# Transposing fp32 activation rows by one fp16 hi/lo DMA per item instead of four TensorE transposes

## The reference, cut to what matters

```
h   = layernorm(x)                                  # per row, eps 1e-5
z   = h @ ctx[e].T                                  # e = min(id clipped to 24999 // 6250, 3)
y   = (silu(z) * z) @ ctx[e]                        # Wg, Wu and Wd are all ctx, einsum 'bsf,df->bsd'
x   = x + tanh(g_xattn) * y
h2  = layernorm(x)
ffn = h2 @ W_base + b_base + (h2 @ A_s) @ B_s
      + sum over the top 2 of 6 experts: gate_e * (h2 @ A_r[e]) @ B_r[e]
out = x + tanh(g_ffn) * ffn
```

## Time and profile before

| | |
|---|---|
| time, median of 3 runs | 231.47 us (231.07 to 231.64) |
| span of the profiled execution, first to last instruction | 229.7 us |
| time of the profiled execution itself | not recorded apart from the runs above; their median lies 1.8 us over the span |
| mean granted TensorE clock | 0.990 of full speed |
| TensorE matmuls busy | 211.8 us (92% of the span) |
| TensorE weight loads busy | 181.7 us (79%) |
| VectorE busy | 168.1 us (73%) |
| ScalarE busy | 77.2 us (34%) |
| POOL busy | 95.4 us (42%) |

### The profile page before, as it was taken

How to read it: one execution, slowest core, us unless ns; L and a number is a source line. 1 busy time by engine, 2 the same in 40 slices (tenths; PEclk the granted TensorE clock), 3 DMA queues, 4 the chain that set the end, 5 groups by cost and what they waited for, 6 DMA issues and landing times.

```text
span 229.7 us, 4143 instructions
## 1 busy us (share of the span) xinstructions
PE 211.8 (92%) x1203; PEld 181.7 (79%) x1204; DVE 168.1 (73%) x423; ACT 77.2 (34%) x166; POOL 95.4 (42%) x147
## 2 busy tenths in 40 slices
PE   0666999999999999999999999999999999999990
PEld 0325788888888888888888889999999999999990
DVE  5878787777865666555566566768999989999761
ACT  4554334323422122222222216044333344333330
POOL 4887743332223333332100111116666665556742
PEclk9997999999999999999999999999999999999998
DMA  4986082111111111001100000001111111211122
GB/s 126 376 248 212 1 288 72 45 46 46 46 46 46 46 46 40 13 39 46 46 0 0 0 0 0 3 1 47 49 46 46 46 46 46 83 54 46 46 93 91
DMA packets 5994, 15.00 MB, mean 65 GB/s; under 512 B 1073, under 2 KB 1073, under 8 KB 5986
## 3 DMA queue, kind: packets, MB, share of 16 engines
q0 software_dynamic: 2800, 9.18, 12.4%
q1 hardware_dynamic: 2544, 4.21, 5.4%
q10 hardware_dynamic: 642, 1.52, 2.0%
HBM read 10.71 MB, written 4.19 MB: 65 GB/s over the span
## 4 chain that ended last, share of the span: by engine, by line
PE 75%; DVE 10%; issue 6%; POOL 5%; ACT 1%; DMA 1%; POOLq 1%; DVEq 0%
PE z_ps L466 17%; PE y_ps L466 17%; PE y_ps L471 8%; PE z_ps L471 8%; PE hT_ps L476 6%; PE ffn_b L466 4%; PE actT_ps L476 4%; PE ffn_a L466 3%; POOL xg L278 2%; PE ffn_b L471 2%; PE actT_ps L552 2%; DVE bn L845 2%; PE ffn_a L471 2%; POOL lo_onehot L294 2%; DVE hwT L893 1%
## 5 line engine op out<-in xcount | busy, mean ns | idle before, releaser
L269 POOL TENSOR_SCALAR var_eps<-stats 128x1 f32<-128x1 f32 x35 | 7.0, 201 | 107.6 <-DVE stats L757 107.4
L466 PE MATMUL z_ps<-ct_split,hT 128*128 x144 | 39.3, 417 | 1.2 <-ACT hT L349 1.2
L466 PE MATMUL y_ps<-ct_split,actT 128*128 x152 | 39.7, 403 | 0.0
L466 PEld LDWEIGHTS z_ps<-ct_split,hT 128*128 128x128 f32 x144 | 26.7, 195 | 6.5 <-issue 1.5
L466 PEld LDWEIGHTS y_ps<-ct_split,actT 128*128 128x128 f32 x152 | 27.2, 189 | 5.2 <-ACT actT L357 0.2
L357 ACT ACTIVATE actT<-actT_ps 128x512 fp32r<-128x512 f32 x19 | 11.4, 599 | 44.8 <-PE actT_ps L476 44.8
L772 DVE TENSOR_TENSOR act<-z_ps,silu 128x512 f32<-128x512 f32 x18 | 12.5, 692 | 17.8 <-ACT silu L353 17.4
L278 POOL DMA_INDIRECT xg<-x_rows,row_index x19 | 22.4, 1180 | 5.8 <-POOL rstd L272 4.2
L476 PE MATMUL hT_ps<-ident,h 128*128 128x128 f32 x140 | 21.1, 273 | 3.0 <-DVE h L761 3.0
L476 PEld LDWEIGHTS hT_ps<-ident,h 128*128 128x128 f32 x140 | 17.6, 142 | 6.2 <-DVE h L761 3.5
L353 ACT ACTIVATE silu<-z_ps 128x512 f32<-128x512 f32 x18 | 10.8, 599 | 34.3 <-PE z_ps L471 34.3
(11 more groups left out here) (157 smaller groups left out, 419.4 us busy)
## 6 DMA issues: line engine op xcount, KB each, us to landing
ct_stage<-ct SPq DMA_DIRECT2D x4, 1024.0 KB, 8.2
ct_stage<-w_ffn ACTq DMA_DIRECT2D x1, 1260.0 KB
xg<-x_rows,row_index POOLq DMA_INDIRECT x19, 3.6
out<-xg,row_index POOLq DMA_INDIRECT x16
ct_stage<-w_up ACTq DMA_DIRECT2D x1, 226.0 KB
ids_sb<-ids SPq DMA_DIRECT2D x1, 8.0 KB, 1.6
gates_raw<-gates SPq DMA_DIRECT2D x1, 1.0 KB, 2.7
br<-b_router SPq DMA_DIRECT2D x1, 3.0 KB
```

The lines of the kernel that those rows point to most:

```text
L466: nc.tensor.matmul(ps, lhs[:, 0, at], rhs(part), start=(k == 0 and part == 0), stop=False)
```

## The change

Each item's rows are split before they are transposed. `item_norm` writes one of two buffers `hs`, scaled by 2^10 (the factor goes into the root). ScalarE rounds it to fp16 (`h_hi`), VectorE writes the difference in fp16 beside it (`h_lo`), and one transposing DMA from SyncE moves the 128 x 1024 halves into `hT_half`, eight blocks of 128 x 128. ScalarE widens all of it in one instruction into the fp32r operand pair, with the scale taken back (`widen`). The TensorE transposes of h, `hT_hi` and `hT_lo` go away in the item stage; product z waits once, for `hT_ready`. The Fori loops of ScalarE and VectorE are written out, TensorE's goes in steps of two. The order becomes:

```diff
         @block.sync
...
-            for q in range(ITEMS):
+            for q in range(3):
                 sp.wait_ge(x_landed[q], 16)
                 sp.sem_inc(x_ready, 1)
+            for q in range(ITEMS):
+                sp.wait_ge(h_lo_ready, q + 1)
+                sp.dma_start_transpose(hT_half[q % 2][:], h_split[q % 2][:]).then_inc(hT_landed[q % 2], 16)
+                if q + 3 < ITEMS:
+                    sp.wait_ge(x_landed[q + 3], 16)
+                    sp.sem_inc(x_ready, 1)
...
-                root(n, rstd_ready, 4 + n + 1)
+                root(n, rstd_ready, 4 + n + 1, 2.0 ** (-2 * H_POWER))
...
-            def hT_hi(q, to=hT):
-                act_e.wait_ge(hT_done, q + 1)
-                nc.scalar.activation(to[:, 0], hT_ps[:], ACT.Copy).then_inc(hT_hi_ready, 1)
+            def h_hi(q):
+                act_e.wait_ge(h_ready, q + 1)
+                nc.scalar.activation(h_split[q % 2][:, 0:D], hs[q % 2][:], ACT.Copy).then_inc(h_hi_ready, 1)
+
+            def widen(q):
+                act_e.wait_ge(hT_landed[q % 2], 16 * (q // 2 + 1))
+                nc.scalar.activation(hTs[q % 2][:].rearrange("p a n -> p (a n)"),
+                                     hT_half[q % 2][:].rearrange("p b t -> p (b t)"), ACT.Copy,
+                                     scale=2.0 ** -H_POWER).then_inc(hT_ready, 1)
...
-            def item(q):
-                silu_of(q)
-                hT_hi(q + 1)
+            def item(q, bank=z_ps):
+                silu_of(q, bank)
+                if q + 2 < ITEMS:
+                    h_hi(q + 2)
                 actT_hi(q)
+                if q + 2 < ITEMS:
+                    widen(q + 2)
...
-            hT_hi(0)
+            h_hi(0)
+            h_hi(1)
+            widen(0)
             ct_hi(LATE_KEY, 0)
             ct_hi(LATE_KEY, 1)
-            hT_hi(1, to=hT_1)
-            silu_of(0)
-            actT_hi(0)
+            widen(1)
+            item(0)
...
-            def product_z(q):
+            def product_z(q, slot):
                 key = key_of(q)
                 pe.wait_ge(ct_lo_ready, S)
-                pe.wait_ge(hT_hi_ready, q + 1)
-                expert_hi(z_ps, hT, key)
-                pe.wait_ge(hT_lo_ready, q + 1)
-                expert_lo(z_ps, hT, key).then_inc(z_done, 1)
+                pe.wait_ge(hT_ready, q + 1)
+                expert_hi(z_ps, hTs[slot], key)
+                expert_lo(z_ps, hTs[slot], key).then_inc(z_done, 1)
...
-            with pe.Fori(2, ITEMS - 1) as q:
-                product_z(q)
-                transpose_h(q + 1)
-                product_y(q - 1)
-                transpose_act(q)
+            with pe.Fori(2, ITEMS - 1, 2) as q:
+                for slot in range(2):
+                    product_z(q + slot, slot)
+                    product_y(q + slot - 1)
+                    transpose_act(q + slot)
...
-            def hT_lo(q, to=hT):
-                dve.wait_ge(hT_hi_ready, q + 1)
-                tt(to[:, 1], hT_ps[:], to[:, 0].bitcast(F32), ALU.subtract).then_inc(hT_lo_ready, 1)
+            def h_lo(q):
+                dve.wait_ge(h_hi_ready, q + 1)
+                tt(h_split[q % 2][:, D:], hs[q % 2][:], h_split[q % 2][:, 0:D], ALU.subtract
+                   ).then_inc(h_lo_ready, 1)
...
             def item(q, bank=z_ps, first=False, extra_before=False):
...
                 aggregate(stats_ready)
-                hT_lo(q + 1)
                 if first:
                     gates_of_rows()
                 item_norm(q + 2)
                 add_product(q - 1, target_of(q - 1) if extra_before else q - 1)
                 actT_lo(q)
+                h_lo(q + 2)
```

More of the change, by code:

```diff
@@ L87, in build_block @@
         h2T = [hT, hT_1, actT]
+        hTs = (hT, hT_1)
+        hs = (h, sb("h_1", [P, D]))
+        h_split = [sb(f"h_split{slot}", [P, 2 * D], F16) for slot in range(2)]
+        hT_half = [sb(f"hT_half{slot}", [P, 2 * KC, P], F16) for slot in range(2)]
         hw = sb("hw", [P, LORA + 1])
@@ L178, in build_block @@
         stats_ready, rstd_ready, h_ready = sem("stats_ready"), sem("rstd_ready"), sem("h_ready")
-        hT_done, hT_hi_ready, hT_lo_ready = sem("hT_done"), sem("hT_hi_ready"), sem("hT_lo_ready")
+        h_hi_ready, h_lo_ready, hT_ready = sem("h_hi_ready"), sem("h_lo_ready"), sem("hT_ready")
+        hT_landed = [sem(f"hT_landed{slot}") for slot in range(2)]
         z_done, silu_ready, act_ready = sem("z_done"), sem("silu_ready"), sem("act_ready")
@@ L205, in build_block @@
         CONSTS = 12
+        H_POWER = 10
         def cols(tensor, position, width=D):
@@ L265, in _, with root @@
             pool.wait_ge(consts_ready, CONSTS)
-            def root(n, done, step):
-                nc.gpsimd.tensor_scalar(var_eps[:], stats[:, 1:2], EPS, 1.0, ALU.add, ALU.mult
+            def root(n, done, step, divisor=1.0):
+                nc.gpsimd.tensor_scalar(var_eps[:], stats[:, 1:2], EPS, divisor, ALU.add, ALU.mult
                                         ).then_inc(pool_step, 1)
@@ L397, in _ @@
             act_e.dma_start(up_stage, w_up).then_inc(up_loaded, 16)
-            silu_of(1, z_1_ps)
-            hT_hi(2)
-            actT_hi(1)
+            item(1, z_1_ps)
             act_e.wait_ge(w_loaded, 16)
-            with act_e.Fori(2, 2 + KC) as q:
+            for q in range(2, 2 + KC):
                 item(q)
@@ L406, in _ @@
             nc.scalar.activation(up_split[:, 0], up_stage, ACT.Copy).then_inc(w_hi_ready, 1)
-            with act_e.Fori(2 + KC, ITEMS - 1) as q:
+            for q in range(2 + KC, ITEMS - 1):
                 item(q)
@@ L492, in key_of @@
                 return pe.value_load(key_table[0:1, bass.ds(q, 1)], min_val=0, max_val=S - 1)
-            def transpose_h(q):
-                pe.wait_ge(h_ready, q + 1)
-                transpose_chunks(hT_ps, h).then_inc(hT_done, 1)
-            def product_z(q):
+            def product_z(q, slot):
                 key = key_of(q)
                 pe.wait_ge(ct_lo_ready, S)
-                pe.wait_ge(hT_hi_ready, q + 1)
-                expert_hi(z_ps, hT, key)
-                pe.wait_ge(hT_lo_ready, q + 1)
-                expert_lo(z_ps, hT, key).then_inc(z_done, 1)
+                pe.wait_ge(hT_ready, q + 1)
+                expert_hi(z_ps, hTs[slot], key)
+                expert_lo(z_ps, hTs[slot], key).then_inc(z_done, 1)
             def product_y(q, key=None, bank_used=True, between=None):
@@ L568, in product_up @@
                 last.then_inc(up_done, 1)
-            transpose_h(0)
             pe.wait_ge(tables_ready, 1)
@@ L577, in _ @@
             pe.wait_ge(ct_lo_ready, key_0 + 1)
-            pe.wait_ge(hT_hi_ready, 1)
+            pe.wait_ge(hT_ready, 1)
             expert_hi(z_ps, hT, key_0)
-            transpose_h(1)
-            pe.wait_ge(hT_lo_ready, 1)
             expert_lo(z_ps, hT, key_0).then_inc(z_done, 1)
             pe.wait_ge(ct_lo_ready, key_1 + 1)
-            pe.wait_ge(hT_hi_ready, 2)
+            pe.wait_ge(hT_ready, 2)
             expert_hi(z_1_ps, hT_1, key_1)
             transpose_act(0)
-            pe.wait_ge(hT_lo_ready, 2)
             expert_lo(z_1_ps, hT_1, key_1).then_inc(z_done, 1)
-            product_y(0, key_0, bank_used=False, between=lambda: transpose_h(2))
+            product_y(0, key_0, bank_used=False)
             transpose_act(1)
-            with pe.Fori(2, ITEMS - 1) as q:
-                product_z(q)
-                transpose_h(q + 1)
-                product_y(q - 1)
-                transpose_act(q)
-            product_z(ITEMS - 1)
+            with pe.Fori(2, ITEMS - 1, 2) as q:
[3 more added lines that the diff above has]
+                    transpose_act(q + slot)
+            product_z(ITEMS - 1, (ITEMS - 1) % 2)
             transpose_h2(0)
@@ L760, in item_norm @@
                 dve.wait_ge(rstd_ready, q + 1)
-                ts(h[:], cols(xg, q), stats[:, 0:1], rstd[:],
+                ts(hs[q % 2][:], cols(xg, q), stats[:, 0:1], rstd[:],
                    ALU.subtract, ALU.mult).then_inc(h_ready, 1)
-            def hT_lo(q, to=hT):
-                dve.wait_ge(hT_hi_ready, q + 1)
-                tt(to[:, 1], hT_ps[:], to[:, 0].bitcast(F32), ALU.subtract).then_inc(hT_lo_ready, 1)
+            def h_lo(q):
+                dve.wait_ge(h_hi_ready, q + 1)
+                tt(h_split[q % 2][:, D:], hs[q % 2][:], h_split[q % 2][:, 0:D], ALU.subtract
+                   ).then_inc(h_lo_ready, 1)
             def activate(q, bn_sem=None, bn_count=0, bank=z_ps):
@@ L803, in _ @@
             first_rows(1)
-            hT_lo(0)
+            h_lo(0)
             item_norm(1)
+            h_lo(1)
             ct_lo(2, 0)
             ct_lo(2, 1)
-            hT_lo(1, to=hT_1)
             item_stats(2)
@@ L813, in _ @@
             actT_lo(0)
+            h_lo(2)
             def item(q, bank=z_ps, first=False, extra_before=False):
@@ L827, in item @@
                 actT_lo(q)
+                h_lo(q + 2)
```

(6 more changed lines are left out.)

## The result

The changed kernel takes 307.38 us, median of 4 runs (305.96 to 307.97), against 231.27 us for the kernel before on the same chip: a ratio of 1.328, 95% interval 1.324 to 1.332. The forecast was 305, in a range of 272 to 350.

A forecast was written before the change was run, and what follows sets the result against it. TensorE, busy 92% of 229.7 us, bounded the kernel before; afterwards the ring would. Start +10.0, items +57.7, weights +7.5 and end -1.5 give +73.7: span 303.4, with 1.8 around it 305 us, range 272 to 350.

The forecast's parts named there:

- D: Time from h_lo's end until ScalarE sees the transposing DMA's landing: taken as 3.6 us, range about 1.8 to 6.2.
- The ring: Item stage: each silu waits, through ScalarE's order, for a landing; period 6.37 us + D, 9.97 against 6.41; items 1 to 17 +57.7.
- The start: Up to the end of activate(1): 40.9 us instead of 30.87, +10.0, with D in it twice.
- The weights: Items 2 to 5: w_hi and w_lo lengthen each turn by 1.45 us, once more for up_split; with gates_of_rows +7.5.
- The end: From activate(17) through the transposes of act(18): 7.1 us instead of 8.6, -1.5.
- TensorE's share: TensorE's busy share in the profile after: down to about two thirds, idle some 4 us before the transposes of act.
- the tile stage: The stage behind the items: same length as before the change.
- Hidden: Rival, item stage: silu(q+1) doesn't wait for widen(q+2), TensorE bounds at 5.86 us a period; 228 us; 2%.
- Short landing: Rival, transposing DMA: D of 1.6 to 1.9 us, as the 8 KB load; 269 to 274 us; 6%.
- Low clock: Rival, item stage: TensorE stays at 1.2 GHz, 11.4 us a period against 9.97; 328 us; 10%.
- Long landing: Rival, transposing DMA: its eight blocks go one after another, D up to 12.8 us; 470 us; 10%.
- The 0.55 us to be saved: TensorE, item stage: the four transposes of h removed per item, 0.55 us; 10.4 us over 19 items if TensorE stays the bound.

The follow-up runs named there:

- Experiment 1: The changed kernel with ScalarE's widen(q+1) behind silu(q), in place of widen(q+2) ahead of silu(q+1): 253.74 us, ratio 1.096 to the kernel before.
- the control in 10: The kernel before with the load of w_up issued as 112 rows and 1 row: 230.86 us, ratio 0.998.
- Experiment 5: The changed kernel with 12 filler matmuls on TensorE between product y and the transposes of act in each item-loop pass: 306.0 us, ratio 1.325.
- experiments 2: The changed kernel with widen(q+1) behind silu(q) on ScalarE and h_lo(q+2) ahead of actT_lo(q) on VectorE: 245.81 us, ratio 1.061.
- 7: The changed kernel with widen behind silu, h_lo ahead of actT_lo, and items 0 to 3 transposed by TensorE: 230.67 us, ratio 0.998.
- 9: The hybrid of 7 (both reorderings, items 0 to 3 transposed by TensorE) with w_up loaded as 112 rows and 1 row: 227.31 us, ratio 0.984.

## Why the prediction was right, point by point

The mechanism was right. That the total came within 2 us is partly luck: the two largest errors, 6.5 and 6.8 us, have opposite signs. With D at the measured 3.1 the prediction's own sum gives 296 us.

- **The ring.** Right in place and in form. The period is 6.37 + D to within 0.1 us for three values of D: 0.06 gives 6.48, 2.5 gives 8.92, 3.1 gives 9.56. Experiment 1 shows that ScalarE's order closes it.
- **D.** Taken as 3.6 from the gather, measured 3.1. The step that put a SyncE DMA level with a POOL gather was off by half a microsecond, the largest mis-sized term: 16 periods of 9.56 are 153.0, not 159.5, so 6.5 us too much. Its argument was wrong too: it gave POOL 1.18 us of issuing that SyncE hasn't, but SyncE's row for the transposing DMA is 1.23 us long.
- **The start.** activate(1) ended at 40.91, forecast 40.9. This is partly luck: SyncE waits for the gathers of items 0 to 2 ahead of its first DMA, which I had missed, so that DMA went out at 20.56 instead of 19.4, and this 1.2 us stood in for the shorter landings.
- **The weights.** 7.5 forecast for w_hi and w_lo in the ring and gates_of_rows; the four periods from item 2 to 6 are 11.08, 11.03, 11.07 and 11.66, together 6.6 over four of 9.56. The first three are 1.5 over it each, as forecast; the fourth, with `up_split` in it, 2.1, so `up_split` cost 0.6 and not the 1.45 of a further turn.
- **Missed:** the 9.7 us landing of item 3, 6.8 us more in one period. I weighed the rate and the size of a DMA, but not what shared its engines. The 25 GB/s of w_up can be seen in the trace of the kernel before as well, in the DMA view of 27 to 47 us, where it costs nothing that can be told (the control in 10).
- **The end.** 7.1 forecast from activate(17) to the transposes of act(18), 9.4 measured (207.24 to 216.65): z(18) ran at a granted clock of 0.63 in the mean (208.4 to 213.0), 3.07 + 1.74 us instead of 2.65. I had written off the clock inside the ring, rightly, and forgotten it where z leaves the ring. Experiment 5 gives 1.6 us of it back.
- **TensorE's share.** Forecast about two thirds, measured 77%: its matmuls of z take longer at the low clock, 553 ns in the mean instead of 417 for the 144 matmuls of its high passes.
- **Sum:** -6.5 for D, +6.8 for w_up, -0.9 for the weights, +2.3 for the end, +0.4 in the tile stage: 2.1 over the forecast span of 303.4, the measured 305.5.
- **The rivals.** *Hidden*: it decides at D under 0.04, and even 0.06 gave 6.48. *Short landing*: D is 3.1, not 1.6 to 1.9. *Low clock*: it fell, but only for a part of each period (0.84 over mid-stage, 0.63 in z and 1.00 in y), and cost nothing there (experiment 5). *Long landing*: the eight blocks don't go one after another; half of them take 2.5 of 3.1 us. The Trainium skill's 1309 ns for one block (VectorE: DVE Perf Modes, "The three transpose paths") would make that 10.5 us in a row by estimate, which the measurement refutes for blocks within one DMA. The Trainium skill's advice on the same page ("Rules for kernel authors"), to transpose on TensorE where PSUM will do, held for this change; with the other order, the first items on TensorE and w_up's load divided it did not (ratio 0.984). The estimate of 2.6 us for these bytes, worked out from the Trainium skill (DMA: Bandwidth & Descriptors, "Anatomy of one DMA"), whose figures are for DMAs issued by POOL, lay 0.5 us under the 3.1, as far as my gather lay over it.
- **The 0.55 us to be saved** is really 0.46 (6.41 to 5.95), since without a transpose between z and y some 0.1 us of change-over stays.

## What to carry to other kernels

When a DMA takes the place of engine work, first write down, for each engine, what is queued behind the instruction that waits for the landing, and follow it round. Here the data were ready two items ahead, and still each silu waited for a landing, because one instruction stood before it; two instructions moved, the first items left as they were and one load of weights divided turned 33% slower into 1.6% faster.

Ahead of a short DMA on the critical path, look at what else is in flight on the same engines, in the GB/s row. Here a low, flat floor of 20 to 27 GB/s was w_up, and dividing that load took 6.6 us off one landing.

## What the runs showed of the hardware that was not expected

- A load of 113 rows of 2 KB ran at 20 to 27 GB/s and held a transposing DMA up for 9.7 us instead of 3.1; as 112 rows and 1 row it did not (3.1 us). How it did so isn't shown.
- A transposing DMA of 128 x 1024 fp16 from SBUF to SBUF lands in 3.1 us in the kernel after; in experiments 2, 7 and 9, where it is issued some 1.8 us behind the start of a 256 KB gather instead of 2.8, in 3.4 to 3.5 in the median. That the gather is the reason was not tested. With half the columns it takes 2.5.
- Of the transposes of 128 x 128 fp32 on TensorE between two products, each after the first costs 0.11 us. The first takes a slot of 0.23, of which only 0.13 goes when it goes (6.08 to 5.95).
